# Convolution layers as 64x64 products on the four quarters of TensorE's array, two batch pairs at a time

## What is computed

```python
xin = shifted + channel_embed[channel_id][None, None, :]
x = jnp.einsum('ble,he->bhl', xin, in_w) + in_b[None, :, None]
for i in range(n_layers):                      # 6 layers, 64 channels, 3 taps, dilation 2**i
    h = jax.nn.gelu(_causal_conv(x, conv_w[i], conv_b[i], 2 ** i), approximate=False)
    h = jax.nn.gelu(jnp.einsum('bhl,oh->bol', h, pw_w[i]) + pw_b[i][None, :, None], approximate=False)
    x = x + h
h = jax.nn.gelu(jnp.einsum('bhl,oh->bol', x, out1_w) + out1_b[None, :, None], approximate=False)
logits = jnp.einsum('bhl,oh->bol', h, out2_w) + out2_b[None, :, None]
```

## Time and profile before

| | us |
|---|---|
| three runs | 319.04, 322.15, 322.27 |
| median | 322.15 |
| span of the profiled execution | 319.3 |

### The profile page before, as it was taken

How to read it: one execution, slowest core, us unless ns; L and a number is a source line. 1 busy time by engine, 2 the same in 40 slices (tenths; PEclk the granted TensorE clock), 3 DMA queues, 4 the chain that set the end, 5 groups by cost and what they waited for, 6 DMA issues and landing times. The chain is left out here.

```text
span 319.3 us, 6069 instructions
## 1 busy us (share of the span) xinstructions
PE 259.9 (81%) x2155; PEld 176.6 (55%) x2164; DVE 228.1 (71%) x489; ACT 167.2 (52%) x308; POOL 151.8 (48%) x181
## 2 busy tenths in 40 slices
PE   1999989678998998967999989988968958856850
PEld 1888877436686776854556555443445525522450
DVE  4364765844348588786587977334999998899997
ACT  0255554574977594634435345325857749734620
POOL 7990004112356573531616244426996748444740
PEclk9999999966999999979599999756999999999985
DMA  4833130000000000000000000000000000000000
GB/s 105 156 86 74 33 56 0 2 0 0 2 1 2 0 4 0 2 2 0 2 0 3 0 2 2 0 0 1 3 2 1 6 12 2 11 9 0 6 14 16
DMA packets 12107, 4.96 MB, mean 16 GB/s; under 512 B 10894, under 2 KB 11566, under 8 KB 12078
## 3 DMA queue, kind: packets, MB, share of 16 engines
q1 hardware_dynamic: 12078, 4.57, 6.8%
HBM read 4.04 MB, written 0.52 MB: 14 GB/s over the span
## 5 line engine op out<-in xcount | busy, mean ns | idle before, releaser
L1135 PE MATMUL bank<-early 128*128 128x256 f32 (+3 forms) x344 | 74.1, 334 | 4.7 <-DVE early L721 2.3
L379 POOL TENSOR_TENSOR shared<-shared 128x512 f16<-128x512 f32 x48 | 56.1, 1169 | 27.9 <-ACT shared L657 22.4
L1135 PEld LDWEIGHTS bank<-early 128*128 128x128 f32 (+1 forms) x344 | 51.9, 158 | 18.8 <-DVE early L721 3.5
L657 ACT CAST shared<-shared 128x512 f16<-128x512 f32 x48 | 29.5, 615 | 26.9 <-DVE shared L1106 26.7
L1135 PE MATMUL bank<-onehot,w3h 128*128 128x512 f16 x96 | 29.2, 386 | 16.9 <-DVE shared L1106 16.8
L1135 PE MATMUL bank<-qT,shared 128*128 128x256 f32 x112 | 33.7, 415 | 4.2 <-DVE shared L816 3.5
L1106 DVE SCALAR_TENSOR_TENSOR shared<-bank,qT 128x512 f32<-128x512 f32 x48 | 32.4, 684 | 5.5 <-ACT qT L673 3.9
L317 POOL TENSOR_TENSOR stat<-stat,neghalf 128x4 f32<-128x4 f32 x16 | 16.3, 1016 | 35.6 <-DVE stat L790 19.3
L673 ACT ACTIVATE qT<-bank 128x512 f32<-128x512 f32 x48 | 28.7, 597 | 6.9 <-PE bank L1135 6.4
L416 POOL TENSOR_TENSOR oTx<-oT,oTx 128x512 f16<-128x512 f32 x16 | 18.9, 1183 | 22.1 <-ACT oTx L561 22.1
L1135 PE MATMUL bank<-onehot,w1h 128*128 128x512 f16 x96 | 29.1, 386 | 0.0
(11 more groups left out here) (217 smaller groups left out, 525.6 us busy)
## 6 DMA issues: line engine op xcount, KB each, us to landing
early<-in_tcn_w_dram SPq DMA_DIRECT2D x2, 352.0 KB, 4.7
w1s<-in_w1m_dram SPq DMA_DIRECT2D x2, 256.0 KB, 4.1
w1s<-in_w3m_dram SPq DMA_DIRECT2D x2, 256.0 KB, 4.0
out_dram<-L SPq DMA_DIRECT2D x16, 32.0 KB, 1.4
idx<-in_x_dram SPq DMA_DIRECT2D x2, 255.0 KB, 3.9
qw<-in_attn_q_dram SPq DMA_DIRECT2D x2, 128.0 KB, 3.7
hTs<-in_w2m_dram SPq DMA_DIRECT2D x1, 256.0 KB
cos<-in_cos_t_dram SPq DMA_DIRECT2D x2, 96.0 KB, 2.2
```

The costliest lines, as they stand in the source:

```text
L379: nc.gpsimd.tensor_tensor(hhx[:, v % 3, 1, i, :], hh[:, u % RING, :], hhx[:, v % 3, 0, i, :], ALU.subtract).then_inc(S["lo_ready"], 1)
L657: nc.scalar.copy(hhx[:, v % 3, 0, i, :], hh[:, u % RING, :]).then_inc(S["hi_ready"], 1)
L1135: return nc.tensor.matmul(out_, l_, r_, start=a, stop=z, skip_group_check=skip)
```

## The change

The convolution and pointwise weights are no longer block-diagonal. `Wq` holds each 64x64 weight once in partitions 0 to 63 and once in 64 to 127; only the two output weights stay as 128x128 blocks (`Wb`). A *step* s is two batch pairs, 2s and 2s + 1. `conv(l, s)` makes twelve products of 64 rows, 64 columns of weights and 256 columns of data: for each tap, rows 0 to 63 go to bank 2s and rows 64 to 127 to bank 2s + 1, pair 2s to the low and pair 2s + 1 to the high partitions of that bank, so that the four products of a tap use the four quarters of the array. `pointwise(l, s)` is one such group of four, with banks 4 + 2s and 5 + 2s; as it mixes the batch rows the same way once more, they come back in their places.

GELUs and residuals work on a step at once (512 columns instead of 256, half as many instructions), except in the last layer, whose last GELU, residual, `out1` and `logits` stay by pair. In the last layer all convolutions and pointwise products come first now, and DVE makes all four residuals before `logits_out(0)`.

The weight casts on DVE are cut up and placed one between every two residuals. The low parts of `w1` and `w3` (128x1536 each) are made by POOL, ahead of its `w2` casts, as soon as DVE has made the high part. `w3` has a staging tile of its own (in the storage of `qT`), so `w1`, `w3` and `w2` are loaded one behind the other, ahead of the qkv, router, cos, sin and wo loads; the layer-norm vectors `lns` and two loads for `Wb` come ahead of the attention weights. The zeroing of `Wt` (1664 columns on POOL and on DVE) shrinks to the two blocks of `Wb`. The first query output on ACT and the later weight readers wait for the new semaphores.

The diff, cut to its core (long runs of removed lines are cut; they stand in the printed functions above):

```diff
-        bank = [ctx.enter_context(nc.psum_tensor(f"bank{i}", [P, 512], f32)) for i in range(8)]
-        NW, NX = NBLK * P, 4 * (PAD + T)
-        early = sb("early", [P, NW + NX + 2048])
-        Wt = early[:, 0:NW].rearrange("p (n o) -> p n o", o=P)
+        banks = ctx.enter_context(nc.psum_tensor("bank", [P, 8, 512], f32))
+        bank = [banks[:, i, :] for i in range(8)]
+        NQ = NBLK - 2
+        NW, NX = NQ * C + 2 * P, 4 * (PAD + T)
+        early = sb("early", [P, TILES * 6 * P // 2])
+        Wq = early[:, 0:NQ * C].rearrange("p (n o) -> p n o", o=C)
+        Wb = early[:, NQ * C:NW].rearrange("p (n o) -> p n o", o=P)
...
+        w3s = qT[:, :, :, :].rearrange("p a b c -> p (a b c)")[:, 0:CH * P].rearrange("p (j c) -> p j c", c=P)
...
-            for lo, hi, s in ((0, TAPS + 1, "ld_tcn0"), (TAPS + 1, NBLK, "ld_tcn1")):
+            for lo, hi, s in ((0, TAPS + 1, "ld_tcn0"), (TAPS + 1, NQ, "ld_tcn1")):
                 for half in range(2):
                     q = slice(64 * half, 64 * half + 64)
-                    sp.dma_start(Wt[q, lo:hi, q], tw[:, lo:hi, :]).then_inc(S[s], 16)
+                    sp.dma_start(Wq[q, lo:hi, :], tw[:, lo:hi, :]).then_inc(S[s], 16)
                 if lo == 0:
                     for half in range(2):
                         sp.dma_start(bt[64 * half:64 * half + 64, :], tcn_b[:, :]).then_inc(S[s], 16)
+            for half in range(2):
+                q = slice(64 * half, 64 * half + 64)
+                sp.dma_start(Wb[q, :, q], tw[:, NQ:NBLK, :]).then_inc(S["ld_tcn1"], 16)
             sp.dma_start(b2bc[:, :], out2_b[:, :].to_broadcast([P, V])).then_inc(S["ld_tcn1"], 16)
+            for half in range(2):
+                q = slice(64 * half, 64 * half + 64)
+                sp.dma_start(lns[q, 0:1], ln1[:, :]).then_inc(S["ld_lns"], 16)
+                sp.dma_start(lns[q, 1:2], ln2[:, :]).then_inc(S["ld_lns"], 16)
             for half in range(2):
                 q = slice(64 * half, 64 * half + 64)
                 sp.dma_start(qw[q, :, :], attn_q.rearrange("c (a m) -> c a m", m=P)).then_inc(S["ld_attn"], 16)
             sp.dma_start(ew[:, :, :], attn_e.rearrange("(a two) j i -> (two j) a i", two=2)).then_inc(S["ld_attn"], 16)
+            sp.wait_ge(S["memz"], 3)
+            for wm, wr, ws, s in ((w1m, w1r, w1s, "ld_w1"), (w3m, w3r, w3s, "ld_w3")):
+                for half in range(2):
+                    q = slice(64 * half, 64 * half + 64)
+                    sp.dma_start(ws[q, 0:NE, :], wm[:, :, :]).then_inc(S[s], 16)
+                    sp.dma_start(ws[q, NE:CH, :].rearrange("c k (two r) -> c (k two) r", two=2)[:, :, 0:REM],
+                                 wr[:, :, :]).then_inc(S[s], 16)
+            sp.dma_start(w2s[:, :, :], w2m[:, :, :]).then_inc(S["ld_w2"], 16)
+            w2v = w2r.rearrange("r (k two) c -> r k two c", two=2)
+            for half in range(2):
+                sp.dma_start(w2x[64 * half:64 * half + REM, :, 64 * half:64 * half + 64],
+                             w2v[:, :, half, :]).then_inc(S["ld_w2"], 16)
...
-            nc.gpsimd.memset(Wt[64:P, :, 0:64], 0.0).then_inc(S["wt_zero_low"], 1)
+            nc.gpsimd.memset(w1s[:, NE:CH, :], 0.0).then_inc(S["memz"], 1)
+            nc.gpsimd.memset(w3s[:, NE:CH, :], 0.0).then_inc(S["memz"], 1)
+            nc.gpsimd.memset(w2x[:, :, :], 0.0).then_inc(S["memz"], 1)
+            pool.wait_ge(S["memz"], 3)
+            nc.gpsimd.memset(Wb[64:P, :, 0:64], 0.0).then_inc(S["wt_zero_low"], 1)
             pool.wait_ge(S["wt_zero_low"], 1)
-            nc.gpsimd.memset(w2x[:, :, :], 0.0).then_inc(S["memz"], 1)
-            nc.gpsimd.memset(w1s[:, NE:CH, :], 0.0).then_inc(S["memz"], 1)
-            pool.wait_ge(S["memz"], 2)
...
+            for i, (dst, src) in enumerate(((w1h, w1s), (w3h, w3s))):
+                pool.wait_ge(S["w1cast"], i + 1)
+                nc.gpsimd.tensor_tensor(dst[:, 1, :, :], src[:, :, :], dst[:, 0, :, :], ALU.subtract) \
+                    .then_inc(S["wlow_ready"], 1)
+                pool.wait_ge(S["wlow_ready"], i + 1)
             pool.wait_ge(S["w2_scaled"], 2)
...
-            def conv_gelu(l, p):
-                act.wait_ge(S["conv_ps"], PAIRS * l + p + 1)
+            def conv_gelu(l, s):
+                act.wait_ge(S["conv_ps"], 2 * l + s + 1)
                 if l:
-                    act.wait_ge(S["pw_ps"], PAIRS * (l - 1) + p + 1)
-                nc.scalar.activation(hid1[:, p, :], bank[p][:, 0:T], ACT.Gelu,
+                    act.wait_ge(S["pw_ps"], 2 * (l - 1) + s + 1)
+                nc.scalar.activation(hid1[:, 2 * s:2 * s + 2, :], banks[:, 2 * s:2 * s + 2, 0:T], ACT.Gelu,
                                      bias=bt[:, l:l + 1]).then_inc(S["hid_ready"], 1)
-            def pw_gelu(l, p):
-                act.wait_ge(S["pw_ps"], PAIRS * l + p + 1)
+            def pw_gelu(l, s):
+                act.wait_ge(S["pw_ps"], 2 * l + s + 1)
                 if l:
-                    act.wait_ge(S["x_ready"], PAIRS * l + p + 1)
+                    act.wait_ge(S["x_ready"], PAIRS + 2 * (l - 1) + s + 1)
+                nc.scalar.activation(hid2[:, 2 * s:2 * s + 2, :], banks[:, 4 + 2 * s:6 + 2 * s, 0:T], ACT.Gelu,
+                                     bias=bt[:, LAYERS + l:LAYERS + l + 1]).then_inc(S["pw_gelu"], 1)
+            def last_gelu(p):
+                l, s = LAYERS - 1, p // 2
+                act.wait_ge(S["pw_ps"], 2 * l + s + 1)
+                act.wait_ge(S["x_ready"], PAIRS + 2 * (l - 1) + s + 1)
                 nc.scalar.activation(hid2[:, p, :], bank[4 + p][:, 0:T], ACT.Gelu,
                                      bias=bt[:, LAYERS + l:LAYERS + l + 1]).then_inc(S["pw_gelu"], 1)
             act.wait_ge(S["ld_tcn0"], 64)
             for l in range(LAYERS - 1):
-                for p in range(PAIRS):
-                    conv_gelu(l, p)
...
+                for s in range(2):
+                    conv_gelu(l, s)
+                for s in range(2):
+                    pw_gelu(l, s)
+            conv_gelu(LAYERS - 1, 0)
+            conv_gelu(LAYERS - 1, 1)
+            last_gelu(0)
+            last_gelu(1)
             out_gelu(0)
-            pw_gelu(l, 2)
-            conv_gelu(l, 3)
+            last_gelu(2)
             out_gelu(1)
+            last_gelu(3)
             out_gelu(2)
-            pw_gelu(l, 3)
             out_gelu(3)
...
+                if p == 0 and a == 0:
+                    act.wait_ge(S["wlow_ready"], 2)
...
-            def residual(l, p):
-                dve.wait_ge(S["pw_gelu"], PAIRS * l + p + 1)
-                dve.wait_ge(S["conv_ps"], PAIRS * l + p + 1)
+            def residual(l, s):
+                dve.wait_ge(S["pw_gelu"], 2 * l + s + 1)
+                dve.wait_ge(S["conv_ps"], 2 * l + s + 1)
+                x_ = Xp[:, 2 * s:2 * s + 2, PAD:PAD + T]
+                V_.tensor_tensor(x_, x_, hid2[:, 2 * s:2 * s + 2, :], ALU.add).then_inc(S["x_ready"], 1)
+            def last_residual(p):
+                l = LAYERS - 1
+                dve.wait_ge(S["pw_gelu"], 2 * l + p + 1)
+                dve.wait_ge(S["conv_ps"], 2 * l + p // 2 + 1)
                 V_.tensor_tensor(Xp[:, p, PAD:PAD + T], Xp[:, p, PAD:PAD + T], hid2[:, p, :], ALU.add) \
                     .then_inc(S["x_ready"], 1)
                 link(V_.tensor_copy(hi, scratch))
                 link(V_.tensor_tensor(lo, scratch, hi, ALU.subtract))
-            def weights_setup(stage):
-                if stage == 0:
...
+            def query_scale():
+                dve.wait_ge(S["ld_attn"], 48)
+                link(V_.tensor_scalar(qw[:, :, :], qw[:, :, :], ATT_SCALE, None, ALU.mult))
+                link(V_.tensor_copy(qwh[:, 0, :, :], qw[:, :, :]))
+            def query_low():
+                link(V_.tensor_tensor(qwh[:, 1, :, :], qw[:, :, :], qwh[:, 0, :, :], ALU.subtract))
+            def project_split():
+                link(V_.tensor_scalar(ew[:, :, :], ew[:, :, :], ATT_SCALE, None, ALU.mult))
+                link(V_.tensor_copy(ewx[:, 0, :, :], ew[:, :, :]))
+                V_.tensor_tensor(ewx[:, 1, :, :], ew[:, :, :], ewx[:, 0, :, :], ALU.subtract) \
+                    .then_inc(S["wts_ready"], 1)
+                dve.wait_ge(S["wts_ready"], 1)
+            def up_scale(i):
+                ws = (w1s, w3s)[i]
+                dve.wait_ge(S["ld_lns"], 64)
+                dve.wait_ge(S[("ld_w1", "ld_w3")[i]], 64)
+                link(V_.tensor_scalar(ws[:, :, :], ws[:, :, :], lns[:, 1:2], FFN_SCALE, ALU.mult, ALU.mult))
+            def up_high(i):
+                V_.tensor_copy((w1h, w3h)[i][:, 0, :, :], (w1s, w3s)[i][:, :, :]).then_inc(S["w1cast"], 1)
+                dve.wait_ge(S["w1cast"], i + 1)
+            def down_scale():
+                dve.wait_ge(S["ld_w2"], 48)
+                for w in (w2s, w2x):
+                    V_.tensor_scalar(w, w, FFN_SCALE, None, ALU.mult).then_inc(S["w2_scaled"], 1)
+            def qkv_split():
+                dve.wait_ge(S["ld_ffn"], 12 * 16)
```

(123 more changed lines are left out.)

40 lines of the change are left out of this document (7 added, 33 removed).

## The result

| | kernel before | changed kernel |
|---|---|---|
| median of the runs | 322.21 us (4 runs, 319.04 to 329.09) | 327.48 us (4 runs, 325.37 to 327.68) |
| span of the profiled execution | 319.3 | 325.8 |

The ratio of the runs is 1.0187, 95% interval 1.0126 to 1.0248. A ratio here is of the runs within 1.5% of the fastest one of their kernel, and none is given where a kernel has only one such run. The forecast was 318, with a range up to 324. The page of the changed kernel, beside the earlier trace rows: PE has less to do, the span is longer.

The account below looks back on a forecast made before the run. The convolution stack was taken as PE-bound. logits_out(0) moving from 56.9 to 53.3 saves 3.6 us, a removed residual 0.2: 319.3 becomes 315.5 for the profiled execution; the median lies 2.9 above, so 318, range 312.5 to 324.

Parts of the forecast that it names:

- the last sentence of the path: Start: zeroing of Wt, about 1.4 us, is off the path, since PE is busy with the embedding until 11.68.
- blocking between POOL and DVE: DVE instructions on SBUF data wait until POOL's running instruction ends, and the reverse; residuals of layers 3, 4 1.1, 0.9 late.
- A second step: Everything behind the stack's end at 56.89 us only shifts with it; 56.9 becomes 53.3, 3.6 us earlier.
- Four quarters at a time: Convolution stack: four products run side by side; a convolution step takes 1.3 us, PE's layer work falls 6.96 to 3.5.
- The rival of the row halves: Row halves do not run side by side: 7.7 us a layer, logits_out(0) at 62.7, total 328; chance 0.1.
- GELU on 512 columns: Convolution stack, ACT: one GELU over a step of two pairs takes 0.69 us, between bounds 0.596 and 0.95.
- POOL's subtraction: Low parts of w1 and w3, 1536 columns each: about 3.3 us on POOL, twice.
- Layers 1 to 4: Time between convolution starts of successive layers: predicted 5.7, 5.6, 6.6 and 6.4 us.
- The alternation of qkv_split with POOL's casts: Layer 4: POOL's w2 work and qkv_split's four instructions wait on each other; residual(4, 1) ends at 46.9 instead of 43.9.
- layer 0: First convolution at 11.68, first GELU at 14.77, residual(0, 0) ends and conv(1, 0) starts at 17.7; predicted 6.0 us.
- The clock rival: Clock falls in PE's hole before conv(5, 1): last layer costs 3 us more, total 321.3; chance 0.14.
- the likeliest case: The whole forecast path with POOL and DVE blocking each other: 318, own range 315.5 to 320.5; chance 0.55.

Follow-up runs that it names:

- Experiment 4: Changed kernel with the one-hot wait, plus POOL starting its w2 casts and subtractions only after residual(4, 1); 316.2 us, 0.9787 of the kernel before.
- onehot_first: Changed kernel plus one wait: POOL zeroes bdT only after DVE has made both one-hot tiles; 319.86 us median, no ratio given.
- onehot_first with fillers: onehot_first plus unread products: five behind logits(3), five behind prep(0)'s transposes, six ahead of conv(5, 1); 314.53 us, 0.9769 of the kernel before.
- w2_cast_late: Same run as Experiment 4: onehot_first with POOL's w2 casts and subtractions held until after residual(4, 1); 316.2 us, 0.9787 of the kernel before.
- blocks_in_steps: onehot_first with the changed schedule kept but the old 128x128 block-diagonal products put back; 329.62 us, 1.0208 of the kernel before.

## Why the prediction was wrong, step by step

**The step that failed** is the last sentence of the path: "The zeroing of Wt (about 1.4 us on POOL and DVE) is off the path". That these instructions are off PE's path is true. But taking them away moved everything behind them on POOL's list 1.2 us forward, ahead of a DVE instruction that then ends only behind POOL's zeroing (3.62 us instead of 0.48), and that cost 6.6 us before the first convolution. The prediction started its path at 11.68, an assumption from the kernel before, and didn't look at what stood beside the instructions that became earlier. The prediction even had the mechanism, blocking between POOL and DVE, and used it for the subtractions only.

**A second step failed** with it: "I take everything behind it as shifted by what these 56.89 us become". The part from the first L808 on took 3.2 us longer than before (+1.5 and +1.7 in the account). The profiled execution came out 10.3 us above the forecast one (325.8 against 315.5): 6.6 for the start, 3.2 behind the first L808, and 0.4 to 0.5 in between.

**What the rows show of it.** In the changed kernel the first one-hot ends 0.28 us behind POOL's zeroing (6.58 + 3.62 against 6.41 + 3.51), like the residual of the earlier trace rows. A residual beside a zeroing is not held up: in the kernel before one took 425 ns from 18.25, with POOL's MEMSET of mask_s running from 18.01 to 18.54:

```profile
18.01 0.53 POOL L295 MEMSET mask_s<- 128x512 bf16 x1
...
L721 DVE TENSOR_TENSOR early<-early x1: 425/425/425, 18.3 to 18.3; 128x256 f32<-128x256 f32 x1
```

The Trainium skill (SBUF — State Buffer, "Who interferes with whom") says that a tensor_scalar can take DVE's second, shared port and then excludes any GpSimd instruction, while a tensor_tensor with two SBUF inputs contends only with GpSimd's reads. By that rule a MEMSET blocks the one-hot and not the residual; the traces of the two kernels agree, with 3.62 us against 0.48 for the one-hot and an unchanged 0.425 for the residual.

**What held.** With the start put back, the first L808 is at 56.97; the prediction had 53.3 for logits_out(0) and 3.75 behind it, 57.0. Its terms one by one, in the changed kernel:
- Four quarters at a time: 24 passes start within 1.2 us (30.5 to 31.7), each group of four within 20 ns, groups 216 ns apart. The rival of the row halves is out.
- GELU on 512 columns 0.687 (0.69), residual 0.690 (0.68), POOL's subtraction 3.54 (3.3). Layers 1 to 4: 5.17, 5.41, 6.10, 5.78 us between conv starts; predicted 5.7, 5.6, 6.6, 6.4. In layers 1 and 2 most of the difference is the second convolution step, 1.5 to 1.7 us behind the first where I had 1.87.
- The alternation of qkv_split with POOL's casts: conv(5, 1) 4.5 us behind conv(5, 0), predicted 4.9. Experiment 4 shows its cause.

That the sum comes out within 0.1 us is in part luck. In onehot_first, layers 1 to 4 and the wait for conv(5, 1) took 1.2 us less than predicted, and the start, layer 0 and the last layer 0.3, 0.5 and 0.5 more. In the changed kernel the same parts took 2.2 less, and layer 0 and the last layer 1.1 and 1.7 more (layer 0: 7.10 us from the first convolution to conv(1, 0), predicted 6.0). Layer 0 is a term that the prediction had too small: in the changed kernel the records of conv(0, 0) take 0.63 us up to 20.5 us and stand 0.43 us apart from group to group, those of conv(0, 1) take 0.376 and stand 0.216 apart. The kernel before started its first convolution at full pace (33 passes in 7.0 us from 11.68 on).

```profile
L1191 PE MATMUL bank<-early x8: 627/654/682, 18.3 to 18.8; 64*64 64x256 f32 x8
...
L1191 PE MATMUL bank<-early x24: 373/376/377, 20.8 to 21.9; 64*64 64x256 f32 x24
```

**The clock rival came true beside the likeliest case,** and I had given it 0.14 as if it excluded it. Its price in the last layer: conv(5, 1) to logits_out(0) took 8.07 us. In onehot_first with fillers, at full clock there, it took 6.0, so 2.1 of them were the clock (I had said 3):

```profile
46.91 1.96 PE L1192 MATMUL bank<-early 64*64 64x256 f32 x32
...
52.91 0.42 DVE L827 TENSOR_TENSOR L<-bank,b2bc 128x256 f32<-128x256 f32 x1
```

The larger part was not in the prediction at all: a second hole, PE idle between logits(3) and the transposes, which didn't exist while out1(3) and logits(3) came late; the clock then fell 1.0 us behind the first L808 instead of 6.0 (65.06 - 64.04, 66.79 - 60.84), and stayed down for 17 us instead of 10. A stage that gets shorter for PE and not for DVE behind it opens such a hole.

**The median.** The runs of one kernel spread by 2 to 17 us, and the clock's stretches differ from profile to profile. I can account for the profiled executions; how the differences between runs of one kernel come about stays open. So does the last line of the account, +1.7 us from the third L808 to the end: the changed kernel has a stretch at half clock at 266 to 270 us that the kernel before does not have there, but that does not settle it, as w2_cast_late and blocks_in_steps have one of the same length at the same place of the work (254.7 to 258.1 and 266.7 to 270.1) and take 227.4 and 227.2 us for this part, less than the kernel before.

## What to carry to other kernels

Work that is taken off an idle engine still moves everything behind it. List what comes earlier, with its new time and length, and look which instructions of the other engines it now overlaps. When PE's work is halved, ask at once where it will be idle: what the clock then takes back can be as large as the gain, and a few products without a reader are a cheap test of it, read on the stretch and over several runs.
